# Attention operands in four quadrants of 32 partitions, loaded in 4 KB rows, and the next batch's projections in the first third of a batch

## What is computed

```python
x = LN(x)                                     # per token
h = rmsnorm(x, norm_w)
q, k, v = h @ Wq, h @ Wk, h @ Wv              # 16 heads of 8
q_phi = taylor_feature_map(q @ Wqf)           # [1, x, pairs x_i x_j]
k_phi = taylor_feature_map(k @ Wkf)
lin = linear_attention_causal(q_phi, k_phi, v)
win = sliding_window_attention(q, k, v)       # window of 64 keys, softmax
x = x + (concat([lin, win]) @ Wout)           # and the outer residual
x = x + moe(LN(x))                            # 4 MLP and 4 KAN experts, top 2
```

## Time and profile before

| | us |
|---|---|
| median of 3 runs | 1187.79 (1186.19 to 1195.24) |
| span of the profiled execution | 1192.4 |
| of it before the first job of batch 0 | 57.06 |
| attention, eight batches | 57.06 to 605.4 |
| routing tables and experts | 605.4 to 1192.4 |
| PE busy | 887.9 (74%) |
| ACT busy | 552.5 (46%) |
| DVE busy | 521.9 (44%) |
| POOL busy | 509.1 (43%) |

### The profile page before, as it was taken

How to read it: one execution, slowest core, us unless ns; L and a number is a source line. 1 busy time by engine, 2 the same in 40 slices (tenths; PEclk the granted TensorE clock), 3 DMA queues, 4 the chain that set the end, 5 groups by cost and what they waited for, 6 DMA issues and landing times.

```text
span 1192.4 us, 24590 instructions
## 1 busy us (share of the span) xinstructions
PE 887.9 (74%) x8106; PEld 675.3 (57%) x8107; DVE 521.9 (44%) x2114; ACT 552.5 (46%) x744; POOL 509.1 (43%) x647
## 2 busy tenths in 40 slices
PE   2087897968889698898950277777699988996871
PEld 1055675646656466665630145446487877886770
DVE  5161735527364262736322011112466666575440
ACT  1275563636556364665610142332566565474440
POOL 6050433425333252534133648774445554462222
PEclk9599898979989798998975588898798988998886
DMA  2504032130503204040101245556133241242113
GB/s 55 81 2 73 6 84 23 61 46 2 95 11 78 29 28 78 2 96 9 29 27 25 47 76 76 89 78 163 49 90 90 62 123 46 56 118 64 38 11 86
DMA packets 96202, 68.64 MB, mean 58 GB/s; under 512 B 42892, under 2 KB 87114, under 8 KB 94730
## 3 DMA queue, kind: packets, MB, share of 16 engines
q1 hardware_dynamic: 79210, 55.36, 20.7%
q0 software_dynamic: 16832, 11.09, 6.8%
HBM read 46.86 MB, written 21.37 MB: 57 GB/s over the span
## 4 chain that ended last, share of the span: by engine, by line
PE 32%; POOL 18%; issue 17%; DMA 13%; DVE 6%; ACT 6%; SPq 5%; POOLq 1%; another core or an unknown queue 1%; DVEq 0%; ACTq 0%
POOL acc_d L751 8%; DMA stack<-zeros 6%; PE pv L1449 5%; PE pv L1636 5%; DMA acc_d<-stack,srec 4%; PE ring L1609 4%; PE ring L1371 2%; PE ring L1391 2%; ACT Pb L851 2%; PE ring L1460 2%; PE ring L1412 2%; ACT stack L928 2%; DVE masked L1050 2%; PE ring L1416 2%; POOL stack L741 1%
## 5 line engine op out<-in xcount | busy, mean ns | idle before, releaser
L751 POOL DMA_INDIRECT acc_d<-stack,srec x84 | 136.3, 1623 | 136.8 <-DVE stack L1237 98.1
L1050 DVE CUSTOM_DVE_ANT_0 masked<-ring,mask_max 128x192 bf16<-128x192 f32 (+1 forms) x512 | 141.6, 337 | 114.4 <-PE ring L1371 102.4
L1248 DVE SCALAR_TENSOR_TENSOR stack<-stack 128x512 f32<-128x512 f32 x240 | 158.0, 690 | 43.8 <-ACT stack L928 29.1
L692 POOL TENSOR_SCALAR_AFFINE_SELECT Pb<-Pb 128x1024 f32<-128x1024 f32 x64 | 69.0, 1094 | 218.9 <-ACT Pb L851 160.0
L928 ACT ACTIVATE stack<-ring,kprm 128x512 f32<-128x512 f32 x160 | 111.2, 794 | 107.7 <-DVE stack L1248 105.5
L1449 PE MATMUL pv<-Pb,vaug 128*16 128x128 f32 (+3 forms) x2816 | 142.7, 329 | 22.8 <-issue 22.6
L1636 PE MATMUL pv<-stack 128*128 128x128 f32 x1120 | 136.0, 285 | 17.0 <-DVE stack L1248 9.7
L1636 PEld LDWEIGHTS pv<-stack 128*128 128x128 f32 x1120 | 132.9, 200 | 20.9 <-DVE stack L1248 10.6
L1609 PE MATMUL ring<-stack 128*128 128x256 f32 x560 | 136.9, 409 | 6.0 <-issue 3.8
L1609 PEld LDWEIGHTS ring<-stack 128*128 128x128 f32 x560 | 115.3, 208 | 30.2 <-issue 7.7
L857 ACT ACTIVATE Pb<-ring 128x768 f32<-128x768 f32 x128 | 101.2, 812 | 56.9 <-PE ring L1400 55.6
(11 more groups left out here) (204 smaller groups left out, 1279.7 us busy)
## 6 DMA issues: line engine op xcount, KB each, us to landing
stack<-L_ffn_kan_sl_W SPq DMA_DIRECT2D x20, 1024.0 KB
stack<-hl_d SPq DMA_DIRECT2D x72, 128.0 KB
Pb<-L_ffn_mlp_W SPq DMA_DIRECT2D x22, 256.0 KB
hl_d<-hi SPq DMA_DIRECT2D x7, 384.0 KB, 2.3
hl_d<-lo SPq DMA_DIRECT2D x7, 384.0 KB, 2.9
xb<-L_attn_x SPq DMA_DIRECT2D x9, 256.0 KB
acc_d<-res SPq DMA_DIRECT2D x8, 256.0 KB, 2.5
h_d<-h SPq DMA_DIRECT2D x8, 256.0 KB, 3.1
```

What stands on the lines that cost most here:

```text
L751: pool.indirect_dma_start(acc_d, bass.IndirectOffsetOnAxis(ap=srec[:, kind, u, q, 0:1], axis=0), src[:, u % 2, q, :], None, compute_op=ALU ...
L1050: red = dve.tensor_tensor_reduce(masked[:, (NT * n + c) % SLOTS, hh, k0:WQ], slot(job)[:, hh // 2, WQ * (hh % 2) + k0:WQ * (hh % 2 + 1)], ...
L1248: dve.scalar_tensor_tensor(basis[z][:, g % G, :], s_, -1.0, s_, ALU.add, ALU.mult).then_inc(k_bas[z], 1)
```

## The change

- The four row groups of 32 partitions of a stack now hold four heads each: quadrant q has rows 32q to 32q+23 for the products, row 32q+24 for maximum or ones, and four blocks of 512 tokens side by side. A stack is 128 x 2048 f16, and a matmul takes 24 or 25 rows of one quadrant.
- Heads are placed (`quadrant`) so that the two PSUM banks of a job get their heads from two quadrants, and the matmuls are issued so that consecutive ones change quadrant and bank. In W both masks now come first, then the four products. The off-diagonal L jobs hold two heads each, one in each bank, in place of one head over both.
- The weights' columns are permuted at preparation, so that hl_d can be read in rows of 4 KB. A stack is loaded with eight DMAs (16 or 8 rows of 4 KB), 24 a batch in place of 9 with 1 KB rows; the store is six DMAs instead of two. The hi and lo rows alternate.
- Rows of zeros are no longer needed: the clearing of the stacks by DVE and ACT, the copies and the ones/zeros DMAs go; two memsets of one half-sized tile each remain.
- In ORDER the steps stats, aggr, coef, hT, q, k, u, v and stacks of the next batch move to the first third.
- GpSimd's residual also waits for n2_ready.

```diff
+QUAD = 32
+NB = H // 4
 ORDER = """
-M L M L M -ytr L M L M L -ycT M L M M -out L L L M -coef2 L M L +stats M +aggr P +coef L L M L L M L
-M M L -h2norm P L +hT -h2T M L -logit L +q L +k mT Y L L -store P L -choose W W W +u +v -rank P
--total W +stacks +residual W -gapexp W W P W Y W W -weights +xload P W W W W Y W W P -scatter P
++stats M L +aggr M L +coef M -ytr L M L M L -ycT M L M M +hT -out L L L M +q -coef2 L M L +k M P L +u L M +v L L
++stacks M L M M L -h2norm P L -h2T M L -logit L L mT Y L L -store P L -choose W W W -rank P
+-total W +residual W -gapexp W W P W Y W W -weights +xload P W W W W Y W W P -scatter P
 """.split()
+def quadrant(h):
+    n, hh = divmod(h, HG)
+    return 2 * (n % 2) + hh // 2, 2 * (n // 2) + hh % 2
...
-            def load_stack(u, s):
-                for g, part in enumerate(((0, 1, 0), (0, 0, 1), (0, 1, 0))[s]):
-                    sp.dma_start(stack[u][s][DH * g:DH * (g + 1), :].rearrange("d (h t) -> d h t", h=H),
-                                 hl_d[part, :, s, :].rearrange("(h d) t -> d h t", d=DH)
+            def store_halves(bf, s):
+                sp.wait_ge(lo_ready, bf * 3 + s + 1)
+                for part, half in enumerate((hi, lo)):
+                    sp.dma_start(hl_d[s, :, part].rearrange("r (n t) -> r n t", n=NB), half[:, s, :]
+                                 ).then_inc(hl_stored[s], 16)
+            def load_stack(bf, u, s):
+                sp.wait_ge(hl_stored[s], bf * 32 + 32)
+                for j in range(4):
+                    rows = hl_d[s, DH * j:DH * (j + 1)]
+                    pairs = rows[:, 0].unsqueeze(1).to_broadcast([DH, 2, NB * T]) if s == 1 else rows
+                    sp.dma_start(stack[u][s][QUAD * j:QUAD * j + 2 * DH, :], pairs).then_inc(stack_loaded[u], 16)
+                    sp.dma_start(stack[u][s][QUAD * j + 2 * DH:QUAD * j + KR, :], rows[:, 1 if s == 1 else 0]
                                  ).then_inc(stack_loaded[u], 16)
...
-            dve.memset(stack[1][0][:].bitcast(F32), 0.0).then_inc(zeroed, 1)
+            dve.memset(stack[1][1], 1.0)
+            dve.memset(stack[0][1], 1.0).then_inc(ones_rows, 1)
...
-            dve.wait_ge(zeroed, 1)
-            for m in range(3):
-                last = dve.tensor_copy(stack[0][m][:], stack[1][0][:])
-            last.then_inc(stack0_zeroed, 1)
...
+                    def rows(m, h, a, b_, k=KR):
+                        quad, nb = quadrant(h)
+                        return stack[p][m][QUAD * quad:QUAD * quad + k, T * nb + a:T * nb + b_]
...
-                        for bk, o, c in ((0, 0, 0), (1, 0, 1), (1, 256, 2)):
+                        first, part = divmod(j - 2, 2)
+                        for o, c in (((0, 0),), ((0, 1), (256, 2)))[part]:
                             w = T - P * (c + 1)
-                            mm = pe.matmul(slot(job)[:, bk, o:o + w],
-                                           sk[:, HG * n + j - 2, P * c:P * (c + 1)],
-                                           su[:, HG * n + j - 2, P * (c + 1):T], start=True, stop=True)
+                            for bk in range(2):
+                                h = HG * n + 2 * bk + first
+                                mm = pe.matmul(slot(job)[:, bk, o:o + w], rows(1, h, P * c, P * (c + 1)),
+                                               rows(2, h, P * (c + 1), T), start=True, stop=True)
...
                         for bk in range(2):
                             pe.matmul(slot(job)[:, bk, 0:2 * WQ], identb[:],
                                       mask_win[:].rearrange("p a q -> p (a q)"), start=True, stop=True)
-                            for jj in range(2):
+                        for jj in range(2):
+                            for bk in range(2):
                                 h = HG * (n - NHG) + 2 * bk + jj
                                 mm = pe.matmul(slot(job)[:, bk, WQ * jj:WQ * jj + wq],
-                                               sk[:, h, P * c:P * (c + 1)],
-                                               sq[:, h, P * c:P * c + wq],
+                                               rows(1, h, P * c, P * (c + 1), KR + 1),
+                                               rows(0, h, P * c, P * c + wq, KR + 1),
                                                start=False, stop=True, skip_group_check=True)
```

More of the change, by code:

```diff
@@ L214, in transformer_kernel @@
         kconst = sb("kconst", [P, 3, Q4])
-        space = [stack[u][m][:].bitcast(F32) for u in range(2) for m in range(3)]
+        space = [m[:] for m in space]
         space += [Pb[:, 0, 0:4096], Pb[:, 1, 0:4096]]
@@ L440, in load_stacks @@
                 for s in range(3):
-                    load_stack(u, s)
-                clear_shift(u)
-            clear_shift(0)
-            for s in range(3):
-                sp.wait_ge(lo_ready, s + 1)
-                for part, half in enumerate((hi, lo)):
-                    sp.dma_start(hl_d[part, :, s, :], half[:, s, :]).then_inc(first_stored[s], 16)
-            for s in range(3):
-                sp.wait_ge(first_stored[s], 32)
-                load_stack(0, s)
-            sp.sem_inc(hl_stored, 32)
+                    store_halves(bf, s)
@@ L454, in _ @@
+                for s in range(3):
+                    load_stack(bf, u, s)
+            sp.wait_ge(ones_rows, 1)
+            load_stacks(0, 0)
             sp.wait_ge(xres_ready, 1)
@@ L816, in front @@
                     if s == "q" and not (isinstance(bf, int) and bf == 0):
[L817 removed]
+                        for m in range(3):
+                            act.wait_ge(hl_stored[m], bf * 32)
                     act.activation(hi[:, SPLIT.index(s), :], src[:, 0, :], ACT.Copy).then_inc(hi_ready, 1)
@@ L825, in _ @@
                 front(s, 0, 0, FRONT.index(s), 0)
-            act.wait_ge(zeroed, 1)
-            for m in range(1, 3):
-                last = act.activation(stack[1][m][:].bitcast(F32), stack[1][0][:].bitcast(F32), ACT.Copy)
-            last.then_inc(stack1_zeroed, 1)
             act.wait_ge(pads_stored, PAD_DMAS)
@@ L975, in _ @@
             dve.wait_ge(prep_mm, 1)
-            dve.tensor_tensor(m_blk[:], slot(0)[:, 1, 0:P], block[:], ALU.mult).then_inc(prep_dve, 1)
-            dve.wait_ge(zeroed, 1)
-            for m in range(3):
-                last = dve.tensor_copy(stack[0][m][:], stack[1][0][:])
-            last.then_inc(stack0_zeroed, 1)
+            for half in range(2):
+                last = dve.tensor_tensor(by_quadrant(m_blk[:], half), by_head(slot(0)[:, 1, 0:P], half),
+                                         by_head(block[:], half), ALU.mult)
+            last.then_inc(prep_dve, 1)
             def front(s, bf, u, job, i):
@@ L1347, in _ @@
                 front(s, 0, 0, FRONT.index(s), 0, None)
-            for u in range(2):
-                pe.wait_ge(ones_loaded[u], 16)
-            pe.wait_ge(const_ready, 3)
+            pe.wait_ge(const_ready, 2)
             pe.wait_ge(pv_zeroed, 1)
@@ L1357, in batches @@
                     p = u % 2
-                    sq, sk, su = (stack[p][m][:].rearrange("r (h t) -> r h t", h=H) for m in range(3))
+                    def rows(m, h, a, b_, k=KR):
+                        quad, nb = quadrant(h)
+                        return stack[p][m][QUAD * quad:QUAD * quad + k, T * nb + a:T * nb + b_]
                     if s in FRONT:
```

98 lines of the change are left out of this document (45 added, 53 removed).

## The result

The changed kernel takes 1265.53 us (median of 4 runs, 1261.69 to 1268.43) against 1189.42 us for the kernel before: a ratio of 1.065, with an interval of 1.060 to 1.069. It is slower by 6.5%, where 3% faster was forecast. On a second occasion the ratio was 1.067 (e12).

A forecast was written before the change was run, and what follows sets the result against it. PE was taken to bound the kernel, busy 59.43 of 68.7 us a batch. Stack waits -13.1, start -13 and 8 x (-1.5 + 0.3) sum to -35.7 us: 1152 off the median of 1187.79, range 1122 to 1180.

The forecast's parts named there:

- The waits for stacks: PE's idle time before a batch's first job: 13.1 us would go with the loads in the batch's first third.
- The last P: The long P job ending each batch, 8.7 us: expected to stay 8 to 9 us, nothing taken off.
- a W job: One W job on PE, masks, products and two switches: 0.70 us instead of 0.66, +0.8 us for 16.
- The start: Time before batch 0 begins: 13 us less, with 7 and 17 as ends.
- B: The 22.3 us of a batch from the output projection up to mT: -0.5 us a batch.
- A: A batch's first 12.5 us, up to the output projection: no change, 0 us.
- C: The 22.6 us of a batch after mT, set by PE alone, before the last P job: -1.0 us.
- Rival 3: PE's clock falls to 1.2 GHz in B if shorter jobs leave gaps: +110 us, 1262; chance 0.05.
- hT's wait: PE waits at hT for GpSimd's hn, behind the records: 0.7 us in four batches, some 0.3 a batch.
- rival 2: Records land late even without loads, hn 5.9 us later, in four batches 24 us: 1176; chance 0.12.
- rivals 1: Row quadrants don't overlap, products stay serial: +3.6 us a batch, 1191 in all, no change; chance 0.13.
- the far end of 4: Better than forecast: ideal pairing, hidden drains, -7.4 us a batch, 17 at the start: 1099; chance 0.15 with partial forms.

The follow-up runs named there:

- e12: The changed kernel run once more, unaltered, on another occasion: ratio 1.067 to the kernel before.
- e6: The kernel before without its 64 scattered record writes: ratio 0.966.
- e3: The kernel before with only the new ORDER and the wait for n2 that it needs: ratio 1.070.
- e1: The kernel before with the products of jobs M, L and W over 32 rows instead of 128, nothing else changed: ratio 1.093.
- the square: Four kernels compared, few rows against 128 rows with padded k, old against new order: e7 1.018, e12 1.067, e5 0.989, e4 1.028.
- e4: The changed kernel with k padded by zeros so that products run over all 128 rows: ratio 1.028 to the kernel before.
- e5: e4 with the old ORDER: ratio 0.989 to the kernel before.
- e7: The changed kernel with the old ORDER: ratio 1.018 to the kernel before.
- e2: The changed kernel with the two heads of one quadrant issued in a row in jobs M, L and W: ratio 1.065 to the kernel before.
- e10: e5 with the padded stack's clearing at the start moved, half to ScalarE and two pieces later: ratio 0.961 to the kernel before.
- e11: e4 without the 64 scattered record writes: ratio 0.966 to the kernel before.

## Why the prediction was wrong

**Right.** The waits for stacks went. The last P kept its 9 us in this trace, and e6 bears out that the record writes have to do with it, but e12 shows that they alone don't decide it. A switch costs 0.10 us and a W job 0.70. The loads were early enough: in batch 1 the last was issued at 152.4 and mT's row at 155.06, so 2.7 us to spare in that batch where 3 were forecast, and e3 shows the full price when they are not. The start gained 9.6 us (from 57.06, where batch 0 began and ran on, to 47.49, where it goes on now), in the range of 7 to 17, though not by the way forecast: the first product came at 35.85, and the padding then held it.

**The step that failed first: B at -0.5 us and A at 0.** In both the sum priced PE's products at the clock of 1.00 and 0.84 that the kernel before had. B went from 24.4 to 32.3 us, A from 10.4 to 12.8, and C, whose first part runs at 0.82 to 0.87, from 22.6 to 25.1 where -1.0 was forecast. The runs show in its place that the clock itself depends on the rows: in B it fell to 0.71 here and to 0.65 in e1, where nothing but the rows changed. Rival 3 had the mechanism's name and nearly its time (1262, measured 1265.53), at a chance of 0.05. The time is luck: it puts 110 us down to the clock, where the square has 2.9 to 5.2 points (34 to 62 us) for the rows and 3.9 to 4.9 for the order. Its condition was the wrong one. I let the clock fall only if PE's jobs left gaps, and weighed it by PE's busy share of 19.88 in 22.3 us. In e1 there are fewer gaps and the clock falls. From the rows of before the fall could not be seen, since all long products there use 128 rows; but for that very reason "the clock there is 1.00" was no evidence for products over 24.

**The second step: hT's wait at 0.7 us, and with it rival 2.** I took 7.42 us for the landing of the records, from the kernel's end, and put the 13.29 of the earlier trace rows down to the stack loads beside them. (The two aren't measured alike: 7.42 counts from the start of the last issue, 13.29 from its end. From the start, has 14.25, so rival 2's 5.9 us were 6.8.) In the kernel after, no stack load is near, and GpSimd goes on 11.09 us after the end of the last issue:

```profile
197.00 2.14 POOL L677 TENSOR_SCALAR_AFFINE_SELECT Pb<-Pb 128x1024 f32<-128x1024 f32 x2 [11.09 <-issue]
...
202.91 1.74 POOL L623 TENSOR_SCALAR hn<-xb,c 128x128 f32<-128x128 f32 x4 [0.21 <-POOL c L614]
```

hn is ready at 204.65, 16.2 us into the batch, not 11.4, and hT waits 4.07 us there. That it isn't more is the long last P's doing, since PE begins the batch later by it: at 188.48, where e12 begins it at 182.40, with the last record issued at 184.96 and 184.52. In e12, the same kernel with a short last P, hT waits 10.49, 7.43 and 6.98 us in the batches where the kernel after has 4.07, 0.15 and 0.91, at the same low clock. In e4, at the full clock, it is 7.3 to 10.4 us in three of eight batches. Rival 2's price of 24 us is near the 25.7 that e4's three make, and the stalls of DVE and ACT come on top. Rival 2 and rival 3 came true together. I had put them side by side as if one excluded the other.

**The range.** 1122 to 1180 left out rivals 1 and 3 and the far end of 4. No sum over cases with one mishap each holds 1265 except rival 3.

## What to carry to other kernels

Before products are cut to fewer rows, ask what the engine's clock will do: here zeros in 104 of 128 rows were worth more than the time that a pair of row quadrants saved, and a padded operand kept the layout's cheaper loads (large packets) and the clock. And when work is moved ahead, look for the last thing that it waits for on every engine: here GpSimd went on 9.0 to 13.6 us after the last scattered write of a batch (e4), and that sets the earliest place of all that stands behind it.

## What the runs showed of the hardware

- The granted clock of B was 1.00 with products over 128 rows, 0.73 with 64, 0.65 with 32, and 0.64 to 0.71 with pairs over 24, at busy shares of 0.90, 0.94, 0.95 and 0.85 to 0.89. That it follows the rows of the long products is shown; why is not.
- In W jobs two heads in a row in one quadrant, then two in the next, overlapped as well as strictly alternating ones: four products of 192 columns in 0.17 us and a switch, both ways.
- While eight scattered record DMAs were under way, the P job beside them took 8.2 to 9.7 us instead of 2.58 on some occasions (before, after, e5, e7) and 2.58 on others (e2, e3, e4, e10, e12); in e4 and e12 DVE and ACT stood still together, for up to 4.6 and 3.2 us. Without the records (e6, e11) neither was seen. What decides between the two is not shown.
- The same kernel took 1160, 1165, 1189 and 1198 us on four occasions (medians), so a time is compared only within one; where ratios of different occasions are set side by side, as in the square, a point or two is uncertain.
